# Second mask's sum in another PSUM bank, gate spread signalled bank by bank, copies and one addition moved between engines

## The reference

```
sa, ca, ga, sb, cb, gb = split(silu(c) @ wmod)          # c is 2 x 512, wmod 512 x 3072
ga, gb = sign(g) * max(|g|, 0.25)                        # g >= 0 counts as +
h = layernorm(x) * (1 + ca) + sa
w = weight * (sum of mask over each 32 x 32 block > 0)
x = x + ga * (h @ w.T + bias)
h = layernorm(x) * (1 + cb) + sb
x = x + gb * ffn(h)       # silu(lin1(h)) * lin3(h), then lin2; hidden width 1376, each with a rank-16 addition
```

## Time and profile before

| | us |
|---|---|
| median of 3 runs (lowest, highest) | 252.25 (252.08, 252.29) |
| the profiled execution | 252.32 |
| its span | 250.5 |
| TensorE busy | 242.3 |
| VectorE busy | 135.9 |
| ScalarE busy | 89.6 |
| GpSimd busy | 97.3 |

### The profile page before, as it was taken

The page is one execution under the profiler, slowest core; times in us unless marked ns, Lnnn a source line. Parts: engine busy times, 40 slices in busy tenths (PEclk is TensorE's granted clock), DMA queues, the critical chain, the costliest instruction groups (busy, mean ns, idle before and its releaser), DMA issues.

```text
span 250.5 us, 3526 instructions
## 1 busy us (share of the span) xinstructions
PE 242.3 (97%) x1265; PEld 192.8 (77%) x1265; DVE 135.9 (54%) x221; ACT 89.6 (36%) x151; POOL 97.3 (39%) x102
## 2 busy tenths in 40 slices
PE   7799999899999999999999999999999999999993
PEld 6677768787788888888888778888888888888772
DVE  2847899899999744744754631741233123312224
ACT  2376554843324465465422311122112221222110
POOL 1377492326532131230210351497346435643300
PEclk9999999999999999999999999999999999999999
DMA  6999991023224413213217520030000000000005
GB/s 184 345 384 407 413 401 42 3 84 119 51 84 127 126 47 123 84 42 128 84 46 107 45 13 0 38 132 0 0 0 4 0 0 0 4 0 0 0 0 169
DMA packets 13041, 24.02 MB, mean 96 GB/s; under 512 B 1240, under 2 KB 2648, under 8 KB 13024
## 3 DMA queue, kind: packets, MB, share of 16 engines
q1 hardware_dynamic: 12864, 23.65, 30.2%
q10 hardware_dynamic: 160, 0.15, 0.2%
HBM read 21.18 MB, written 2.10 MB: 93 GB/s over the span
## 4 chain that ended last, share of the span: by engine, by line
PE 82%; DVE 6%; DMA 3%; issue 3%; POOL 2%; ACT 1%; SPq 1%; DVEq 0%; POOLq 0%; ACTq 0%
PE up_b L1156 25%; PE up_a L1156 24%; PE acc L1170 8%; PE acc L1171 8%; PE acc L1169 8%; DMA wmod_sb<-in_wmod 3%; PE side L1137 2%; DVE xt L839 1%; DVE stats L699 1%; PE acc L999 1%; DVE wa L813 1%; PE side L1141 1%; DVE xt L818 1%; PE acc L1106 1%; POOL ht_lo L419 1%
## 5 line engine op out<-in xcount | busy, mean ns | idle before, releaser
L940 DVE TENSOR_TENSOR g<-up_b,g 128x512 f32<-128x512 f32 (+1 forms) x22 | 15.2, 690 | 64.5 <-PE up_b L1156 64.5
L1170 PE MATMUL acc<-w_lo,g_hi 128*128 128x512 f32 (+1 forms) x88 | 34.7, 394 | 0.0
L1171 PE MATMUL acc<-w_hi,g_lo 128*128 128x512 f32 (+1 forms) x88 | 34.7, 394 | 0.0
L1169 PE MATMUL acc<-w_hi,g_hi 128*128 128x512 f32 (+1 forms) x88 | 34.6, 394 | 0.0
L670 ACT ACTIVATE g<-up_a 128x512 f32<-128x512 f32 (+1 forms) x22 | 13.1, 597 | 58.8 <-PE up_a L1156 58.5
L827 DVE SCALAR_TENSOR_TENSOR raw<-side,raw 128x512 f32<-128x512 f32 (+2 forms) x33 | 21.5, 676 | 22.3 <-PE side L1137 15.7
L677 ACT ACTIVATE g_hi<-g 128x512 fp32r<-128x512 f32 (+1 forms) x22 | 13.9, 633 | 49.4 <-DVE g L940 49.4
L462 POOL TENSOR_TENSOR w_lo<-work,w_hi 128x512 fp32r<-128x512 f32 (+1 forms) x11 | 14.2, 1287 | 41.1 <-ACT w_hi L604 41.1
L597 ACT ACTIVATE w_hi<-raw 128x512 fp32r<-128x512 f32 (+2 forms) x33 | 20.3, 626 | 21.2 <-DVE raw L827 21.1
L944 DVE TENSOR_TENSOR g_lo<-g,g_hi 128x512 fp32r<-128x512 f32 (+1 forms) x22 | 22.9, 1041 | 8.7 <-ACT g_hi L677 8.4
L1156 PE MATMUL up_a<-ht_hi,w_lo 128*128 128x512 f32 (+1 forms) x88 | 24.2, 396 | 0.4 <-DVE w_lo L833 0.4
(11 more groups left out here) (172 smaller groups left out, 379.3 us busy)
## 6 DMA issues: line engine op xcount, KB each, us to landing
raw<-in_ffn SPq DMA_DIRECT2D x33, 256.0 KB, 2.7
wmod_sb<-in_wmod SPq DMA_DIRECT2D x4, 1024.0 KB, 11.5
xt<-in_x SPq DMA_DIRECT2D x8, 256.0 KB, 8.2
wmod_sb<-in_wmod SPq DMA_DIRECT2D x1, 2048.0 KB, 15.1
out<-xt SPq DMA_DIRECT2D x8, 256.0 KB, 2.7
mask_sb<-in_mask SPq DMA_DIRECT2D x4, 256.0 KB, 9.2
wa<-in_weight SPq DMA_DIRECT2D x4, 256.0 KB, 9.2
lora_raw<-in_lora SPq DMA_DIRECT2D x1, 512.0 KB, 10.4
```

What stands on the lines that cost most here:

```text
L940: nc.vector.tensor_tensor(g[0:w], up_b[0:w], g[0:w], ALU.mult).then_inc(g_ready, 1)
L1169: nc.tensor.matmul(acc[t][:], hi, down_hi[j][0:w], start=(j == 0), stop=False)
L1170: nc.tensor.matmul(acc[t][:], hi, down_lo[j][0:w], start=False, stop=False)
L1171: last = nc.tensor.matmul(acc[t][:], lo, down_hi[j][0:w], start=False, stop=(j == HT - 1))
```

## The change

- `mask_bank`: the second mask's sum goes to `acc[3]` instead of `side[0]`. The bias product waits for the first comparison only, `mask_blocks(1)` stands behind `attend_bias(0)`, `turn(3)` (which writes `acc[3]`) comes after the second comparison and ahead of `mod_products(0, 1)`; `mask_blocks(2)` stands behind `attend(0, 0, 1)` instead of ahead of it, `mask_blocks(3)` behind `attend(0, 1, 1)` instead of ahead of `attend(0, 1, 0)`.
- `gate_spread` goes bank by bank in the order of `TURN_BANKS` and signals after each bank.
- The four gate copies are shared: ScalarE takes banks 1 and 2, VectorE 0 and 3. ScalarE's stand between its first lora part and the second one, which is moved ahead of `high(4)`.
- VectorE's `gates_of(0)` stands ahead of `centres(T)`; its `lora_part(1)` goes from between `columns` and `centres(2T + 2)` to behind `lora_part(0)`.
- The fourth addition of batch 0 is GpSimd's, behind `low(7)` and ahead of the roots of the second norm, and waits for VectorE's three.
- The loads keep their order.

```diff
-X1_POOL = (4, 5, 6, 7)
+X1_POOL = (3, 4, 5, 6, 7)
-GATE_COPIES = T
+GATE_COPIES = T // 2
+        gate_row_by_act = sem("gate_row_by_act")
         def mask_bank(k):
-            return acc[1] if k >= 2 else side[0]
+            return (side[0], acc[3], acc[1], acc[1])[k]
             def add_x1(n):                                   # GpSimd
                 b, t = divmod(n, T)
                 pool.wait_ge(attn_gated, n + 1)
+                if n < T:
+                    pool.wait_ge(x1_by_dve, n)
...
             low(KT + 3)
+            add_x1(T - 1)
             root(2 * T, 2)
...
+            def gate_copy(q):                                # ScalarE
+                act.wait_ge(spread_out, TURN_BANKS.index(q) + 1)
+                act.wait_ge(block_on_ready, KT)
+                src = acc[q][:, 2 * P:(2 + B) * P].rearrange("p (b n) -> p b n", b=B)
+                nc.scalar.activation(mask_sb[:, 0:B, q * P:(q + 1) * P].bitcast(F32), src, ACT.Copy
+                                     ).then_inc(gate_row_by_act, 1)
...
             lora_high(0)
+            for q in TURN_BANKS[0::2]:
+                gate_copy(q)
+            lora_high(1)
             high(4)
...
-            for n in range(1, len(LORA_CUTS)):
+            for n in range(LORA_FIRST, len(LORA_CUTS)):
                 lora_high(n)
...
             def gate_copy(q):                                # VectorE
-                dve.wait_ge(spread_out, 1)
+                dve.wait_ge(spread_out, TURN_BANKS.index(q) + 1)
...
             moment(7)
+            gates_of(0)
             centres(T)
-            gates_of(0)
             norm(T + 2)
             norm(T + 3)
-            for q in TURN_BANKS:
+            for q in TURN_BANKS[1::2]:
                 gate_copy(q)
             lora_part(0)
+            lora_part(1)
             whole(4)
...
             add_x1(2)
-            add_x1(3)
...
             columns()
-            lora_part(1)
             centres(2 * T + 2)
...
                 if i == 1:                                   # turn
-                    pe.wait_ge(gate_row_ready, k + 1)
+                    pe.wait_ge(gate_row_ready if k % 2 else gate_row_by_act, k // 2 + 1)
...
-                for b in range(B):                           # gate_spread
-                    for q in range(KT):
-                        rows = slice(q * QUAD, (q + 1) * QUAD)
+                for q in TURN_BANKS:
+                    rows = slice(q * QUAD, (q + 1) * QUAD)
+                    for b in range(B):
                         row = q * QUAD + b
                         last = nc.tensor.matmul(...)
-                last.then_inc(spread_out, 1)
+                    last.then_inc(spread_out, 1)
...
             fill(FILL_H)                                     # TensorE's list
-            mask_blocks(1)
             pe.wait_ge(ones_ready, 1)
             pe.wait_ge(bias_ready, 1)
             pe.wait_ge(cols_ready, 1)
+            pe.wait_ge(block_on_ready, 1)
+            attend_bias(0)
+            mask_blocks(1)
+            attend(0, 0, 0)
             pe.wait_ge(block_on_ready, 2)
-            attend_bias(0)
-            attend(0, 0, 0)
+            turn(3)
             mod_products(0, 1)
-            turn(3)
+            attend(0, 0, 1)
             mask_blocks(2)
-            attend(0, 0, 1)
             first_columns(1)
             attend(0, 0, 2)
-            mask_blocks(3)
             attend(0, 1, 0)
             attend(0, 1, 1)
+            mask_blocks(3)
             attend(0, 1, 2)
             attend(0, 2, 0)
```

More of the change, by code:

```diff
@@ L809, in attn_gate @@
                 dve.wait_ge(gate_row_ready, GATE_COPIES)
+                dve.wait_ge(gate_row_by_act, GATE_COPIES)
                 if b:
@@ L1086, in attend_bias @@
                     pe.wait_ge(gate_row_ready, GATE_COPIES)
+                    pe.wait_ge(gate_row_by_act, GATE_COPIES)
                 for t in ts:
```

## The result

The changed kernel takes 252.77 us (median of 12 runs, 252.56 to 253.08) against 252.12 for the kernel before on the same chip: ratio 1.0025, 95% interval 1.0017 to 1.0034. It is slower by 0.65 us, where 0.95 had been forecast.

What follows compares the result with a forecast made beforehand. Bound: the joint TensorE, VectorE, ScalarE, GpSimd chain ahead of TensorE's 60.56 matmul. Bias -0.4 absorbed, masks +1.5, ScalarE's queue +0.15, addition and hold -0.85, collision and turns +0.1 to 0.2: +0.95, 253.2 us, range 252.8 to 253.7.

Steps and rivals of the forecast that it cites:

- First mask and collision: At the first masks: bias starts 0.4 us earlier, second mask's sum +0.55, mask_weight(1) loses SBUF access to GpSimd, ending +1.55.
- Rival 1: At mask_weight(1): VectorE wins the access at 15.5, the 0.88 block goes, end +0.1 (252.3); chance 0.14.
- Rival 4: At the bias: new bank doesn't free it, start 15.06 or later, end within 0.3 of forecast; chance 0.05 within forecast's 0.52.
- How it goes on: Later masks after the first collision: VectorE loses to GpSimd again, masks +1.5, carried through norms to batch 1's turns, +1.5.
- The hold at `mask_weight(3)`: GpSimd's low part of the third weight holds SBUF access to 23.35; VectorE ends at 23.9 instead of 22.39, +1.5.
- Norms and turns of batch 1: VectorE's norms 28.18 to 29.7, turns 29.66 to 31.15; TensorE stands 1.7 us, +1.5.
- The sign that a norm would end it: Ahead of batch 1's turns: a TensorE stall over 1 us, released by ScalarE's or VectorE's norm.
- Shared copies: ScalarE's queue ahead of high(4): two copies of 0.39 and second lora high; first high +1.6, wholes +1.65 (+0.15 in the sum).
- Fourth addition and last root: Before second norms: addition saves 0.60 and the hold was already paid, +1.65 becomes +0.8; root step gives 0.56, little shows.
- addition and hold: VectorE's additions before the second statistics: 0.60 from the moved addition, rest from the hold already paid, -0.85 in the sum.
- Rival 3: GpSimd's first spread beats VectorE's second lora part at 32.0; VectorE waits 0.5 to 0.6 longer, end 253.75; chance 0.17.
- Rival 2: ScalarE and GpSimd catch up before the norms; addition and root clear the turns' 0.65 stall, end 251.6; chance 0.17.

## Why the prediction was right

**First mask and collision: right.** The bias started at 13.91 with the fill ending at 13.98, near the upper bound as taken, and the mask's sum 0.44 after the bias. From the first product to `mask_weight(1)` it took 4.15 us (14.99 - 10.84) against 3.51 before (14.95 - 11.44): +0.64, where +0.55 was forecast. GpSimd came first by 0.13 us. The margin had been put at 0.17, and GpSimd's own start moved too, by 0.12 from the first product (14.86 - 10.84 against 15.34 - 11.44), so the side of the race was a near thing, as the prediction said. Removing the collision gave 0.74 back; putting the bias ahead of the sum, which brings it in, cost 0.8 to 0.9. Rival 1 is what the run with the waiting low part comes close to: its 0.9992 is 0.2 us under the time before, where the rival had 0.1 above it. The block that this rival puts at 0.88 is 1.0 by the prediction's own numbers (17.19 - 15.5 - 0.69), and 1.01 was measured (1.70 - 0.69). Rival 4 did not come: the bias started at 13.91, ahead of the second comparison.

**How it goes on: right in its end, not in one part.** The hold at `mask_weight(3)` had been counted and did not happen. Its sum came 0.33 later than forecast (22.13 - 10.84 = 11.29 against 22.4 - 11.44 = 10.96), so VectorE asked just as GpSimd let go, and GpSimd's release set the end all the same: counted from the first product it ended at 12.54 (22.67 + 0.71 - 10.84), against 10.95 (22.39 - 11.44) before, +1.6 with 1.5 forecast.

**Norms and turns of batch 1.** The turns started at 30.72 (+1.06, or +1.66 from the first product; +1.5 forecast). The load of x landed so that the statistics started at 24.19, not 23.8; this was one execution's landing, as in the other profiles they started at 22.54 to 23.65. Forecast was a stall of 1.7 us at the turns; there were two, 0.63 at the spread and 0.76 at the turns, and one of 1.50 in the run with the second lora part back. The sign that a norm would end it did not come: ScalarE's first gate copy did (30.72 [0.76 <-ACT mask_sb L623]), while VectorE's norms had ended at 30.16 (29.16 + 1.00).

**Shared copies: a wait and a gain that the prediction did not have.** It charged ScalarE's queue with +0.15 ahead of the first high, and gave the two copies saved on VectorE no value, since VectorE "is not what is late here". The two copies on ScalarE took 0.63 us together, not 2 x 0.39. From the first product the first high came 1.66 later (31.39 - 10.84 against 30.33 - 11.44), as much as the turns, so the queue added nothing behind them; it stood ahead of them instead, as the first copy is behind ScalarE's first lora part. Copies ahead of that lora part were not tried.

That VectorE was not late holds for its wholes: in the kernel before they started at 31.14, as ScalarE's first high (from 30.33, 0.78 long) ended at 31.11. But VectorE's copies and first lora part come one behind the other, and GpSimd's two spreads wait for that lora part:

```profile
29.10 1.41 DVE L790 COPY mask_sb<-acc 128x256 f32<-128x256 f32 x4
30.43 0.60 DVE L797 SCALAR_TENSOR_TENSOR parts<-parts,const,lora_raw 128x384 fp32r<-128x384 f32 x1
```

```profile
31.14 1.21 POOL L430 TENSOR_SCALAR b<-parts,half_on 128x128 fp32r<-128x128 f32 x2 [2.99 <-DVE parts L797]
32.32 2.53 POOL L419 TENSOR_TENSOR ht_lo<-hbuf,ht_hi 128x512 fp32r<-128x512 f32 x2
```

In the run with the copies alone:

```profile
30.23 1.21 POOL L431 TENSOR_SCALAR b<-parts,half_on 128x128 fp32r<-128x128 f32 x2 [2.33 <-DVE parts L811]
31.62 2.54 POOL L420 TENSOR_TENSOR ht_lo<-hbuf,ht_hi 128x512 fp32r<-128x512 f32 x2 [0.18 <-DVE hbuf L750]
```

Before, GpSimd's spreads end where its first low part begins, though VectorE's first whole was done at 31.94 (31.14, and 0.80 for one); with the copies shared they are out of the way, and the low part waits for the whole alone. The last low part ends 7.68 us after the start of the turns before (36.05 + 1.29 - 29.66) and 7.47 after it here (35.36 + 1.29 - 29.18). This is a reading of two traces; that it is the whole gain of the copies is not shown.

Alone, the shared copies are worth 0.28 us (0.9988, 0.9980 to 0.9997), and about 0.3 when taken out again (0.9991 against 0.9981). This is as large as the difference between 0.95 and 0.65, but it was measured without the collision, and in the profile of the changed kernel the spreads, held up by the second lora part, end at 33.22, no sooner than the low part begins. Counted from the first product that profile has +0.86 at 60.82, next to the forecast's +0.94. Where the 0.3 us between forecast and medians went stays open; it is no more than what two single profiles of kernels with the same median can differ by (0.35, last section).

**Fourth addition and last root: sizes right, value none.** The additions took 2.50 instead of 3.28, the root step 0.23 instead of 0.78, GpSimd's addition (40.12 to 41.41) ended 0.9 us before the fourth statistics, as forecast. But the sum took -0.85 for addition and hold, and without the collision taking the addition out again moved nothing; with the collision in it was not tried. Either of addition and lora part clears the stall of 0.65 ahead of the turns of the second norms. With both undone it is back at 0.45 (the copies alone) and the time at 251.83 against 251.5 to 251.6 with one of them, though these intervals overlap. Past the stall TensorE's own queue is the limit. So the forecast's end came by TensorE's path in it (+1.65 less the stall of 0.65), whatever the addition gave. In the changed kernel even the lora part is worth nothing, since TensorE comes late by itself; that last part the prediction had.

**Rival 3** (a third collision, GpSimd's first spread against VectorE's second lora part) did not come: VectorE went on from one lora part to the next without a break (30.75, 1.40 for both), and GpSimd's spread was the one held, 1.76 us instead of 1.21. **Rival 2** gave the time of the rest of the change well (251.68 with the masks undone, 251.6 forecast), but not with the masks in it, and its number is right in part by luck: it had the stall cleared by the addition and the root together, where either alone does it.

**What the page says of the port pair.** By the Trainium skill ("SBUF — State Buffer", "Who interferes with whom") the first to issue holds the pair for its whole instruction. The traces agree on who waits: a lead of 0.13 us decided over 1.01 us. That the loser then runs its whole 0.69 us, as the prediction read the rule, is not what they show: VectorE ended 0.56 and 0.55 us after the release, as in the trace of before.

## What to carry to other kernels

Two engines that exclude each other make a race out of every start time: before moving an operation later by half a microsecond, look in the trace at what the other engine starts within that half microsecond, and count what is left of the other's operation as the price (1.01 us here), plus what is queued behind. If the race is lost, a wait that keeps the less urgent operation back can be cheaper than the collision (0.74 us here). Savings that clear the same stall don't add up, so each is to be measured with the others in and out. And a copy moved to another engine stands behind what that engine already has in its list: look at what waits for the copy there too.

## What had not been expected

The start of the first product varied from 10.8 to 11.4 us between profiles with the landing of one load, as much as the whole effect. Two single profiles compared by their absolute times would have given +0.3 us; counted from that product, +0.86; the medians of 12 runs say +0.65. Counting from the first product is no exact measure either: the kernel with the gates alone moved has its up product 49.47 us behind it (60.59 - 11.12), the kernel before 49.12 (60.56 - 11.44), at medians that don't differ. VectorE kept the pair over two operations in a row while GpSimd was waiting for it: 1.40 us for both lora parts, with the spread held for 0.55 us.
